# First attention of a four-layer kernel: the exponentials moved up in ScalarE's order, k, oT and v behind them, the value projection in the o bank, and both blocks of transposed P copied out by ScalarE

## The chip, the core and the metric

The program runs on one core of a Trainium2 chip. TensorE (PE) multiplies into PSUM, which the kernel addresses as eight banks of 512 fp32 columns; VectorE (DVE), ScalarE (ACT) and GpSimd (POOL) work beside it, and SyncE (SP) issues the DMAs. Every engine executes its own instructions in its own order, and the engines wait for each other on semaphores only. The metric is the device time of one execution, in microseconds (us).

## What is computed

Four layers of attention and feed-forward on x of 16 items by 256 rows by 128 features (`mod` comes from a small matrix product; `_layernorm` and `softmax` are the usual ones). The change is in the attention of the first layer, for 16 heads of 64 features:

```
h = _layernorm(x, axis=-1) * (1 + ca) + sa
x = x + ga * _L0_attn_ref(h, L0_attn_Wq, L0_attn_Wkv, L0_attn_Wo, L0_attn_bo)
...
q, k, v = heads of x @ Wq, x @ Wkv
s = jnp.einsum('bhid,bhjd->bhij', q * scale, k)
gm = jax.lax.stop_gradient(jnp.max(s, axis=-1, keepdims=True))
p = jnp.where(causal_mask, 0.0, jnp.exp(s - gm))
out = einsum('bhij,bhjd->bhid', p, v) / (jnp.sum(p, axis=-1, keepdims=True) + EPS)
return out.transpose(0, 2, 1, 3).reshape(B, N, H * Dh) @ Wo + bo
```

(The q, k, v line is shortened here.) The later layers, with their own attentions and mixtures of experts, are the same in both kernels.

## The kernel before

`attention0` works in steps. A step is one pair of heads of one item: 8 steps per item, 16 items, 128 steps with step numbers s and place p = s mod 8 in the item. `walk` calls each engine's `step(at)` for a lead-in of 6 empty steps and the first 16 steps written out, then for a hardware loop whose body (a lap) is 16 steps, then for the last 16 steps and `LAG` steps of drain. In a step, `at` is the current pair, `nx` the next, `b1`, `b2` and `b3` the pairs one, two and three steps back. The order of the calls in `step` is the order of the instructions on the engine, so the work is a software pipeline written out by hand:

- TensorE (lines 531 to 600): the transposes of P for `b2` (helper line 403), the score products of `at` (line 549), the projections of q, of v and of k for `nx` (helper lines 123 to 125, three multiplies each, because the operands are cut into two parts of reduced precision, "rounded" and "rest"), the causal mask of head 0 added into the score bank (571, 573), the product with the values for `b2` (586, "o"), the mask of head 1, and the output projection of `b3` (598, "y"). At p = 5 the transposes of the next item's normalised rows (535, "ht") come first.
- ScalarE (lines 482 to 519): the copies of oT of `b3` (498) and of the second block of transposed P (502) out of PSUM, the rounded parts of q and k for `nx` (513), v (515), and then the exponentials of head 0 and head 1 (488 and 490, two ACTIVATEs per head, each followed by a read of its row sums). At p = 5 it also writes hT (409) and its rounded part (132); at p = 3 it copies the finished sum y of an item (214).
- VectorE (lines 616 to 652): the first block of transposed P (623), the negated row maxima of both heads (628), the denominators (636, 638), the scaling of P (643, four instructions), and the rest parts of q and k (651). At p = 2 it normalises rows of a later item (172), at p = 4 it takes the statistics of the finished item (233).
- GpSimd (lines 461 to 470): three TENSOR_TENSORs per item on the sum taken at p = 3 (221, 224, 226: bias, gate, residual), and at p = 5 the rest part of hT (139).

PSUM before: banks 0 and 1 hold q and k in their first halves; the second half of bank 0 holds ht, that of bank 1 holds v. Banks 2 and 3 hold the scores of the two heads, banks 4 and 5 their transposed P (384 of 512 columns), bank 6 holds o (256 columns used), bank 7 holds y. A score product of the next step (549) waits for two things: both heads' exponentials of the step before (it overwrites the score banks), and q and k of its own pair with their rest parts.

## Time and profile before

| | us |
|---|---|
| three runs | 2811.14, 2815.62, 2815.95 |
| median | 2815.62 |
| the profiled execution, its own time | 2808.51 |
| span of its trace | 2806.8 |
| score products of the first attention, first to last start | 46.4 to 668.3 |

Over the whole span TensorE is busy 90%, VectorE 70%, ScalarE 50% and GpSimd 24%. These shares are averages over eight stages that have different limits; the change touches the first only, which lasts from about 46 to 672 us. Times in the trace count from the start of the span. The profiled execution was 7.1 us shorter than the median of the three runs.

### The profile page before, as it was taken

The page shows a single profiled execution, that of the slowest core. Times are in us where ns is not written, and L with a number is a line of the kernel's source. Part 1 is how long each engine was busy: PE and PEld are TensorE (multiplying, and loading weights), DVE is VectorE, ACT ScalarE, POOL GpSimd, SP SyncE. Part 2 cuts the span into 40 slices and gives each one's busy share as a digit, 9 for nine tenths or more (in the row PEclk, how much of TensorE's full clock was granted, in tenths as well). Part 3 has the DMA queues.
Part 4 walks back from the last instruction along what each step waited for, and adds up shares of the span by engine and source line. Part 5 has one row for each costly group of instructions (what it writes and reads, how often), then busy time and mean ns, then how long its engine had stood idle before and what let it go on. Part 6 is the DMA issues. An engine that isn't in the chain of part 4 may idle for free. (4 is left out here: it accounts for less than half of the span.)

```text
span 2806.8 us, 65268 instructions
## 1 busy us (share of the span) xinstructions
PE 2535.8 (90%) x20904; PEld 2129.8 (76%) x20904; DVE 1971.7 (70%) x6148; ACT 1416.5 (50%) x4025; POOL 660.1 (24%) x1195
## 2 busy tenths in 40 slices
PE   4999999997999989999996999968997886999888
PEld 3777777776888879999996999956665464666566
DVE  4878878786777568888885777756775225777687
ACT  3777777775555445565654322314554132555544
POOL 0000000000111100001100111146774025777322
PEclk9999999998999999999998999979998897999899
DMA  5000000002000245555554000037553754655100
GB/s 147 2 2 0 1 1 1 1 1 62 4 0 0 59 142 169 165 170 170 168 167 108 2 0 0 0 116 191 151 152 89 84 55 109 168 147 150 37 14 17
DMA packets 196168, 212.10 MB, mean 76 GB/s; under 512 B 12628, under 2 KB 179940, under 8 KB 194676
## 3 DMA queue, kind: packets, MB, share of 16 engines
q1 hardware_dynamic: 195956, 209.64, 28.2%
q8 instruction: 88, 1.44, 0.2%
q14 instruction: 124, 1.02, 0.1%
HBM read 108.95 MB, written 90.65 MB: 71 GB/s over the span
## 5 line engine op out<-in xcount | busy, mean ns | idle before, releaser
L628 DVE TENSOR_REDUCE a_nmax<-bank 128x2 f32<-128x512 f32 x256 | 164.9, 686 | 98.9 <-PE bank L549 98.9
L1098 ACT ACTIVATE a_p<-a_p,a_nmax 128x256 f32<-128x256 f32 x256 | 128.3, 502 | 209.1 <-DVE a_nmax L1286 205.3
L221 POOL TENSOR_TENSOR delta<-y,arena 128x256 f32<-128x256 f32 x32 | 24.7, 772 | 787.9 <-ACT y L214 787.9
L1734 ACT ACTIVATE a_p<-bank 128x1024 f32<-128x1024 f32 (+1 forms) x256 | 193.4, 808 | 23.7 <-PE bank L1789 19.1
L1362 ACT ACTIVATE f_silu<-bank 128x512 f32<-128x512 f32 x128 | 76.5, 597 | 214.5 <-PE bank L125 214.5
L820 ACT ACTIVATE f_hidden<-bank,arena 128x256 f32<-128x256 f32 x256 | 120.3, 472 | 114.8 <-PE bank L125 113.5
L513 ACT CAST a_qk<-bank 128x256 fp32r<-128x256 f32 x256 | 95.0, 374 | 163.3 <-PE bank L125 163.3
L883 PE MATMUL bank<-arena,f_hidden 128*128 128x128 f32 x1024 | 171.6, 288 | 6.4 <-DVE f_acc L937 5.2
L139 POOL TENSOR_TENSOR hT<-hT 128x256 fp32r<-128x256 f32 x64 | 47.0, 734 | 523.5 <-ACT hT L132 481.9
L1677 POOL TENSOR_SCALAR_AFFINE_SELECT a_p<-a_p 128x512 f32<-128x512 f32 x256 | 162.9, 636 | 0.0
L937 DVE SCALAR_TENSOR_TENSOR f_acc<-bank,f_cw,f_acc 128x128 f32<-128x128 f32 x448 | 134.8, 345 | 38.8 <-PE bank L883 36.1
L1943 DVE TENSOR_REDUCE a_nmax<-bank 128x4 f32<-128x1024 f32 x128 | 155.5, 1215 | 2.7 <-PE bank L1776 2.7
L123 PE MATMUL bank<-hT,f_w 128*128 128x256 f32 x512 | 156.0, 305 | 0.3 <-POOL hT L139 0.3
L883 PEld LDWEIGHTS bank<-arena,f_hidden 128*128 128x128 f32 x1024 | 136.6, 191 | 19.5 <-DVE f_acc L937 11.3
L124 PE MATMUL bank<-hT,f_w 128*128 128x256 f32 x512 | 145.4, 284 | 0.0
L125 PE MATMUL bank<-hT,f_w 128*128 128x256 f32 x512 | 145.3, 284 | 0.0
L1217 PE MATMUL bank<-a_v,a_pT 128*128 128x128 f32 x1024 | 138.1, 278 | 3.7 <-ACT a_pT L1081 3.6
L549 PE MATMUL bank<-a_qk 64*128 64x256 f32 x1536 | 126.2, 295 | 15.7 <-ACT a_p L490 5.4
L1217 PEld LDWEIGHTS bank<-a_v,a_pT 128*128 128x128 f32 x1024 | 131.7, 193 | 6.6 <-ACT a_pT L1081 5.4
L1417 PE MATMUL bank<-arena,f_hidden 128*128 128x128 f32 x1024 | 136.0, 276 | 0.0
L549 PEld LDWEIGHTS bank<-a_qk 64*128 64x128 f32 x1536 | 102.5, 187 | 40.7 <-DVE a_qk L651 27.4
L1292 DVE TENSOR_TENSOR a_pos<-bank,arena 128x384 f32<-128x384 f32 x256 | 130.7, 551 | 2.7 <-PE bank L125 2.4
(321 smaller groups left out, 8210.9 us busy)
## 6 DMA issues: line engine op xcount, KB each, us to landing
pos_dram<-a_pos SPq DMA_DIRECT2D x128, 383.0 KB, 2.8
a_stack<-rows_dram SPq DMA_DIRECT2D x128, 320.0 KB, 4.1
rows_dram<-a_cut SPq DMA_DIRECT2D x192, 192.0 KB, 2.4
a_shifted<-pos_dram SPq DMA_DIRECT2D x128, 256.0 KB, 2.7
f_merged<-f_staged SPq DMA_DIRECT2D x16, 578.0 KB, 9.0
gate<-gates_dram SPq DMA_DIRECT2D x32, 256.0 KB, 11.0
arena<-in_task SPq DMA_DIRECT2D x4, 1156.0 KB, 7.8
x<-in_x SPq DMA_DIRECT2D x4, 512.0 KB, 8.3
```

The lines of the kernel that those rows point to most:

```text
L123: pe.matmul(out, left[0], right[0], start=start, stop=False, skip_group_check=True)
L124: pe.matmul(out, left[0], right[1], start=False, stop=False, skip_group_check=True)
L125: return pe.matmul(out, left[1], right[0], start=False, stop=stop, skip_group_check=True)
L549: mm = pe.matmul(s_ps[h][:, t * T:(t + 1) * T], qk[64 * h:64 * h + 64, at.ring(2), 0, a, t * P:(t + 1) * P], qk[64 * h:64 * h + 64, at.rin ...
L628: dve.tensor_reduce(nmax[:, at.ring(2), h, :], s_ps[h][:].rearrange("p (t k) -> p t k", t=NT), AX_X, ALU.max, negate=True).then_inc(s["nma ...
L883: mm = pe.matmul(y, hidden[:, at.ring(2), t * P:(t + 1) * P], w["e2w"][:, at.p, :], start=(t == 0), stop=not last, skip_group_check=True)
L937: i = dve.scalar_tensor_tensor(out=a, in0=z, scalar=c[:, t, at.p:at.p + 1], in1=a, op0=ALU.mult, op1=ALU.add)
L1217: mm = pe.matmul(y[:, t * P:(t + 1) * P], pT[:, b2.ring(2), j, t * P:(t + 1) * P], v[:, slot, j, h * P:(h + 1) * P], start=(b2.p == 0 and ...
L1417: mm = pe.matmul(y_ps[at.ring(2)][:, t * P:(t + 1) * P], hidden[:, at.ring(2), c * T + t * P:c * T + (t + 1) * P], w["w3"][:, at.p, c, :], ...
L1677: pool.affine_select(blocks, blocks, [[0, 4], [1, P]], ALU.is_ge, 0.0, base=0, channel_multiplier=-1).then_inc(s["causal"], 1)
L1734: act.activation(p[:, b4.ring(2), first:end], sT_ps[:, first:end], ACT.Exp).then_inc(s["exp"], 1)
L1943: dve.tensor_reduce(nmax[:, half, 1, of], s_ps[:, 2 * T:6 * T].rearrange("p (c q) -> p c q", c=4), AX_X, ALU.max, negate=True).then_inc(s[ ...
```

## The change

In words, for each engine:

- **PSUM.** v is now projected into the second half of bank 6, beside o; ht goes into the last 128 columns of banks 4 and 5, beside transposed P.
- **ScalarE.** A step now reads: both blocks of transposed P of `b2`, rounded q, exponentials of head 0, rounded k, exponentials of head 1, oT of `b2` (of the step's own o, no longer of the one before), v. hT moves from p = 5 to p = 4, between transposed P and q, its rounded part to the end of that step. The copy of y moves from the start of p = 3 to the end of p = 2.
- **TensorE.** v is projected first, then q, then k. The v projection waits until ScalarE has copied the v and the oT before it. The ht transposes come at p = 4, and wait for nothing of q or k.
- **VectorE.** It no longer copies transposed P. Normalising and statistics go to the end of their steps, the statistics from p = 4 to p = 3; the rest of k waits for rounded k itself, and no longer for v, which came after it.
- **GpSimd.** Bias, gate and residual are written at p = 2, where the sum is taken now; `LAG` is 4.

```
-        o_ps, y_ps = k.banks[6], k.banks[7]
+        o_ps, v_ps, y_ps = k.banks[6][:, 0:T], k.banks[6][:, T:2 * T], k.banks[7]
+        ht_ps = k.psum.rearrange("p (b c) -> p b c", b=8)[:, 4:6, C:512]
...
-        LAST, LEAD, LAG = PER - 1, 6, 5
+        LAST, LEAD, LAG = PER - 1, 6, 4
...
-                    if at.p == 3 and at.shift(-4).real:
-                        biased_residual_by_pool(pool, n, at.shift(-4), k.gate[phase % 2],
+                    if at.p == 2 and at.shift(-3).real:
+                        biased_residual_by_pool(pool, n, at.shift(-3), k.gate[phase % 2],
...
                     if b2.real:
+                        wait(act, s["pT_mm"], b2, 2, 1)
+                        wait(act, s["o_mm"], b2.shift(-2))
+                        act.copy(pT[:, b2.ring(2), 0, :], pT_ps[0][:, 0:C]).then_inc(s["pT0"], 1)
                         wait(act, s["pT_mm"], b2, 2)
                         wait(act, s["o_mm"], b2.shift(-2))
                         act.copy(pT[:, b2.ring(2), 1, :], pT_ps[1][:, 0:C]).then_inc(s["pT1"], 1)
...
+                    ni = at.shift(4)
+                    if at.p == 4 and ni.real:
+                        wait(act, s["ht_mm"], ni, item=True)
+                        wait(act, s["pT0"], b2)
+                        modulated(act, k, phase, ni, ht_ps, n.hT[:, ni.s // PER % 2, :].rearrange("p (t q) -> p t q", t=NT),
+                                  s["ht"])
...
+                        rounded(nx, 0)
                     if at.real:
                         exps(0)
+                    if nx.real:
+                        rounded(nx, 1)
                     if at.real:
                         exps(1)
+                    if b2.real:
+                        wait(act, s["o_mm"], b2)
+                        wait(act, s["y_mm"], b2.shift(-2))
+                        act.copy(oT[:, b2.ring(2), :], o_ps).then_inc(s["oT"], 1)
+                    if nx.real:
+                        wait(act, s["v_mm"], nx)
+                        wait(act, s["o_mm"], nx.shift(-7 - nx.p % 2))
+                        act.copy(v[:, nx.s // 2 % 4, nx.p % 2, :], v_ps).then_inc(s["v"], 1)
+                    if at.p == 4 and ni.real:
+                        cut_hT(act, n, ni, s["ht"], s["ht_rounded"])
+                    if at.p == 2 and b3.real:
+                        take_sum(act, n, b3, y_ps, s["y_mm"], s["biased"], s["taken"])
...
-                    if at.p == 5 and ni.real:
+                    if at.p == 5:
+                        wait(pe, s["ht"], at.shift(3), item=True)
+                    ni = at.shift(4)
+                    if at.p == 4 and ni.real:
                         wait(pe, s["xn"], ni, item=True)
-                        wait(pe, s["qk"], at, 2, 1)
...
+                        wait(pe, s["v"], nx.shift(-1))
+                        wait(pe, s["oT"], b3)
+                        matmul3(pe, v_ps, halves(n.hT2, item, t * P, (t + 1) * P),
+                                [W[:, 2, part, first:first + 2 * P] for part in range(2)]).then_inc(s["v_mm"], 1)
...
-                    if b2.real:
-                        wait(dve, s["pT_mm"], b2, 2, 1)
-                        wait(dve, s["o_mm"], b2.shift(-2))
-                        dve.tensor_copy(pT[:, b2.ring(2), 0, :], pT_ps[0][:, 0:C]).then_inc(s["pT0"], 1)
...
-                    if at.p == 4 and at.shift(-5).real:
-                        row_stats(dve, n, at.shift(-5), s["added"])
...
+                    if at.p == 3 and at.shift(-4).real:
+                        row_stats(dve, n, at.shift(-4), s["added"])
```

ScalarE in a step of the loop without extras, before (from the rounded q to the second block of transposed P; L68 rows are register or semaphore instructions of `wait`):

```order
L513 CAST a_qk<-bank 128x256 [waits a0_qk_mm]
L68 REGISTER_ALU
L513 CAST a_qk<-bank 128x256 [waits a0_qk_mm]
L515 COPY a_v<-bank 128x256 [waits a0_o_mm]
L488 ACTIVATE a_p,a_sums<-bank,a_nmax 128x128 [waits a0_pT_mm,a0_masked,a0_nmax]
L490 ACTIVATE a_p,a_sums<-bank,a_nmax 128x256
L488 ACTIVATE a_p,a_sums<-bank,a_nmax 128x128 [waits a0_pT_mm,a0_masked,a0_nmax]
L490 ACTIVATE a_p,a_sums<-bank,a_nmax 128x256
L498 COPY a_oT<-bank 128x256 [waits a0_y_mm,a0_o_mm]
L502 COPY a_pT<-bank 128x384 [waits a0_o_mm,a0_pT_mm]
```

The same stretch of ScalarE's order in the changed kernel, from the second of the two copies of transposed P on (the lines are those of the changed kernel: 504 transposed P, 486 rounded q and k, 493 and 495 exponentials, 523 oT, 527 v):

```order
L504 COPY a_pT<-bank 128x384 [waits a0_o_mm,a0_pT_mm]
L68 ISA [waits a0_s_mm]
L486 CAST a_qk<-bank 128x256 [waits a0_qk_mm]
L493 ACTIVATE a_p,a_sums<-bank,a_nmax 128x128 [waits a0_pT_mm,a0_masked,a0_nmax]
L495 ACTIVATE a_p,a_sums<-bank,a_nmax 128x256
L68 REGISTER_ALU
L486 CAST a_qk<-bank 128x256 [waits a0_qk_mm]
L493 ACTIVATE a_p,a_sums<-bank,a_nmax 128x128 [waits a0_pT_mm,a0_masked,a0_nmax]
L495 ACTIVATE a_p,a_sums<-bank,a_nmax 128x256
L523 COPY a_oT<-bank 128x256 [waits a0_y_mm,a0_o_mm]
L68 REGISTER_ALU
L527 COPY a_v<-bank 128x256 [waits a0_o_mm,a0_v_mm]
```

Rounded k stands between the two heads' exponentials now, and oT and v stand behind both.

TensorE before, from the output projection at the end of p = 4 over the ht transposes to the first projection of p = 5 (`pro_mod_mm` and `pro_gate_abs` are the printed names of reused semaphores, here xn and ht):

```order
L598 MATMUL bank<-arena,a_oT 128x128 [waits a0_oT]
L598 MATMUL bank<-arena,a_oT 128x128
L68 REGISTER_ALU
L68 ISA [waits pro_mod_mm]
L535 MATMUL bank<-ident,xn 128x128 [waits a0_qk]
L535 MATMUL bank<-ident,xn 128x128
L403 MATMUL bank<-ident,a_p 128x128 [waits a0_pT1,a0_pT0,a0_p]
L403 MATMUL bank<-ident,a_p 128x128 x5
L68 REGISTER_ALU
L549 MATMUL bank<-a_qk 128x256 [waits a0_exp,a0_qk]
L549 MATMUL bank<-a_qk 128x256 x11
L123 MATMUL bank<-hT,a_W 128x256 [waits a0_qk,pro_gate_abs]
```

TensorE in the changed kernel, the same place, now one step earlier (550 is ht, 564 the scores, 612 the output projection; the last row is the first multiply of v):

```order
L612 MATMUL bank<-arena,a_oT 128x128 [waits a0_taken,a0_oT]
L612 MATMUL bank<-arena,a_oT 128x128
L68 REGISTER_ALU
L550 MATMUL bank<-ident,xn 128x128 [waits a0_pT1,a0_pT0,pro_mod_mm]
L550 MATMUL bank<-ident,xn 128x128
L403 MATMUL bank<-ident,a_p 128x128 [waits a0_pT1,a0_pT0,a0_p]
L403 MATMUL bank<-ident,a_p 128x128 x5
L68 ISA
L564 MATMUL bank<-a_qk 128x256 [waits a0_exp,a0_qk]
L564 MATMUL bank<-a_qk 128x256 x11
L68 REGISTER_ALU
L123 MATMUL bank<-a_W,hT 128x256 [waits a0_oT,a0_v]
```

The transposes no longer wait for the rest part of q, and the projections that follow wait for oT and v instead of for q and hT.

VectorE before, p = 4, from the row maxima to the first scaling of P:

```order
L628 TENSOR_REDUCE a_nmax<-bank 128x2 [waits a0_exp,a0_s_mm] x2
L233 ISA [waits a0_added]
L233 REGISTER_ALU
L233 BN_STATS row_stats<-x 128x6
L233 ISA
L233 BN_STATS row_stats<-x 128x6
L68 REGISTER_ALU
L636 TENSOR_SCALAR a_den<-a_sums 128x4 [waits a0_exp]
L638 RECIPROCAL a_rec<-a_den 128x4 [waits a0_den]
L643 TENSOR_SCALAR a_p<-a_p,a_rec 128x128 [waits a0_rec]
```

VectorE in the changed kernel, from the rest of k at the end of p = 3 into p = 4 (636 row maxima, 642 denominators, 654 rest parts):

```order
L654 TENSOR_TENSOR a_qk<-bank,a_qk 128x256 [waits a0_qk_rounded]
L233 ISA [waits a0_added]
L233 REGISTER_ALU
L233 BN_STATS row_stats<-x 128x6
L233 ISA
L233 BN_STATS row_stats<-x 128x6
L68 REGISTER_ALU
L636 TENSOR_REDUCE a_nmax<-bank 128x2 [waits a0_exp,a0_s_mm] x2
L642 TENSOR_SCALAR a_den<-a_sums 128x4 [waits a0_exp]
```

The statistics left the stretch between the maxima and the scaling, and stand between the rest of k and the next maxima.

## Rows read from the trace of the kernel before

**Rows 1.** Busy time of each engine in a stretch, then granted clock, DMA share, GB/s.
```profile
400.00:600.00 200.00, 190.76 (x1779) 155.11 (x1777) 160.50 (x473) 141.99 (x552) 14.67 (x20) 1.00 0.00 1
```

**Rows 2.** TensorE in time order: start, us, engine, line, tiles, [idle before]; score products of s = 32 to 40, and s = 48.
```profile
204.99 0.98 PE L549 MATMUL bank<-a_qk 64*128 64x256 f32 x12
210.51 0.98 PE L549 MATMUL bank<-a_qk 64*128 64x256 f32 x12
...
219.86 0.97 PE L549 MATMUL bank<-a_qk 64*128 64x256 f32 x12
224.83 0.98 PE L549 MATMUL bank<-a_qk 64*128 64x256 f32 x12
230.26 0.97 PE L549 MATMUL bank<-a_qk 64*128 64x256 f32 x12
235.14 0.97 PE L549 MATMUL bank<-a_qk 64*128 64x256 f32 x12
239.94 0.98 PE L549 MATMUL bank<-a_qk 64*128 64x256 f32 x12 [0.24 <-ACT a_p L490]
244.62 0.98 PE L549 MATMUL bank<-a_qk 64*128 64x256 f32 x12
...
283.20 0.97 PE L549 MATMUL bank<-a_qk 64*128 64x256 f32 x12
```

**Rows 3.** ScalarE in time order, step s = 39, which has no extras.
```profile
241.50 0.37 ACT L513 CAST a_qk<-bank 128x256 fp32r<-128x256 f32 x1 [1.07 <-PE bank L125]
242.21 0.37 ACT L513 CAST a_qk<-bank 128x256 fp32r<-128x256 f32 x1 [0.33 <-PE bank L125]
242.48 0.38 ACT L515 COPY a_v<-bank 128x256 f32<-128x256 f32 x1
242.74 0.38 ACT L488 ACTIVATE a_p<-bank,a_nmax 128x128 f32<-128x128 f32 x1
...
243.54 0.38 ACT L488 ACTIVATE a_p<-bank,a_nmax 128x128 f32<-128x128 f32 x1
...
244.24 0.23 ACT L490 ACTIVATION_READ_ACCUMULATOR a_p<-bank,a_nmax 128x1 f32 x1
```

**Rows 4.** TensorE in the same step: end of the first mask, transposes of P.
```profile
242.08 0.22 PE L573 MATMUL bank<-causal_bf,ident_bf 128*128 128x128 bf16 x1
...
243.66 0.85 PE L403 MATMUL bank<-ident,a_p 128*128 128x128 f32 x6
```

**Rows 5.** VectorE in the same step: denominators, scaling of P, rest parts.
```profile
242.16 0.16 DVE L636 TENSOR_SCALAR a_den<-a_sums 128x4 f32<-128x4 f32 x1
...
242.57 1.01 DVE L643 TENSOR_SCALAR a_p<-a_p,a_rec 128x128 f32<-128x128 f32 x4
243.49 0.75 DVE L651 TENSOR_TENSOR a_qk<-bank,a_qk 128x256 fp32r<-128x256 f32 x2
```

**Rows 6.** ScalarE's copy of y, GpSimd's first and third operation, VectorE's denominators, s = 35.
```profile
219.57 0.40 ACT L214 COPY y<-bank 128x256 f32<-128x256 f32 x1
...
220.12 0.73 POOL L221 TENSOR_TENSOR delta<-y,arena 128x256 f32<-128x256 f32 x1 [27.04 <-ACT y L214]
...
221.96 0.73 POOL L226 TENSOR_TENSOR x<-x,delta 128x256 f32 x1 [0.19 <-POOL delta L224]
...
222.07 0.64 DVE L636 TENSOR_SCALAR a_den<-a_sums 128x4 f32<-128x4 f32 x1
```

**Rows 7.** Around the start of s = 37: VectorE's statistics, TensorE's ht, ScalarE's pT and hT.
```profile
227.05 0.48 DVE L233 BATCH_NORM_STATS2 row_stats<-x  x2
...
229.24 0.44 PE L535 MATMUL bank<-ident,xn 128*128 128x128 f32 x2 [0.53 <-DVE a_qk L651]
...
230.37 0.48 ACT L502 COPY a_pT<-bank 128x384 f32<-128x384 f32 x1 [0.75 <-PE bank L403]
230.75 0.57 ACT L409 ACTIVATE hT<-bank,mod 128x256 f32<-128x256 f32 x1
```

**Rows 8.** ScalarE's first instruction after the loop's branch, s = 32.
```profile
206.83 0.37 ACT L498 COPY a_oT<-bank 128x256 f32<-128x256 f32 x1 [1.96 <-issue]
```

More of the change, by code:

```diff
@@ L482, in step, with rounded @@
                     nx, b1, b2, b3 = at.shift(1), at.shift(-1), at.shift(-2), at.shift(-3)
+                    def rounded(nx, i):
+                        wait(act, s["qk_mm"], nx, 2, 1 - i)
+                        act.copy(qk[:, nx.ring(2), i, 0, :], qk_ps[i][:, 0:T]).then_inc(s["qk_rounded"], 1)
                     def exps(h):
```

38 lines of the change are left out of this document (7 added, 31 removed).

## The prediction

> **What bounds the kernel now.** I read the busy time by stretches first, then the start times of the score products, and then the engines in time order within one step. The change lives in the first attention, so only that stage counts. There TensorE is busy 190.76 of 200 us at a granted clock of 1.00 [rows 1]: whatever the change does, little more than its remaining 5% and a few waits can be won. The score products mark the steps. The first item of the lap takes 244.62 - 204.99 = 39.63 us, the second 283.20 - 244.62 = 38.58, the lap 78.21 [rows 2]. The first item's steps are 5.52 (p = 0, after the loop's branch), twice 4.68, 4.97 (p = 3), 5.43 (p = 4), 4.88 (p = 5), 4.80 (p = 6) and 4.68 (p = 7). So a plain step costs 4.68, and an item about 2 us on top for its extras.
>
> What closes a plain step? I give times in s = 39 from its score product at 239.94 [rows 2]. ScalarE is free until q is there (it idled 1.07 before 1.56), rounds k at 2.27, copies v at 2.54, starts the exponentials of head 0 at 2.80 and of head 1 at 3.60, and its last read of sums ends at 244.24 + 0.23, at 4.53 [rows 3]. The next score product starts at 4.68, 0.15 later. The other two rings are shorter: VectorE's rest parts end at 4.30 [rows 5], and TensorE starts transposing P at 3.72 [rows 4]. ScalarE's chain from k to the second exponential is what ends last, by 0.15 to 0.2.
>
> **The change, plain steps.** The first mask ends at 242.08 + 0.22, at 2.36 [rows 4]. Head 0's exponentials could start then, but stood behind k and v until 2.80. In the new order the walk is: mask 2.36; start of head 0 at 2.43 (TensorE to ScalarE takes 0.04 where the rounded k follows its multiply, and a second semaphore has to be looked at; I take 0.07); 0.80 for a head (242.74 to 243.54) gives 3.23; rounded k, slot 0.27 (242.21 to 242.48), gives 3.50; head 1 to its last read, 243.54 to 244.47, is 0.93, gives 4.43; plus 0.15 is 4.58 [rows 3]. So v's slot of 0.26 and the early start are worth 0.36, the k that now stands between the heads gives back 0.27, and **0.10 per plain step** is left.
>
> Next in line: VectorE. In s = 35 its chain was 0.47 late (denominators ended at 222.71, at 2.85, against 242.32, at 2.38, in the plain step), and the step came out at 4.97, so without that delay it would allow 4.97 - 0.47 = 4.50 [rows 2, 5, 6]. TensorE: 8 transposes before the score product of s = 37 took 230.26 - 229.24 = 1.02 for ht and P together; six take some 0.75 to 0.8 of it, and from 3.72 this gives 4.47 to 4.5 [rows 2, 4, 7]. Both lie under 4.58 by less than 0.1. That is also the most a plain step could win beyond my forecast.
>
> The new copies. The first block of transposed P costs ScalarE a slot of 0.38 (230.37 to 230.75) [rows 7]; it takes at most its 0.48 of duration. What follows the last exponential starts 0.29 before the next score product (the copy of y at 219.57, before 219.86 [rows 2, 6]). There now stand oT and v (0.27 each) and two copies of transposed P (0.38 each): the last is issued by 1.01. q is rounded after that, and later than before: the two roundings are 0.71 apart for six multiplies (241.50 to 242.21), so v's three multiplies ahead of q move it from 1.56 to 1.92 [rows 3]. hT at p = 4 adds 0.6 there and ends at 1.6: hidden. The product with the values needs transposed P only behind the first mask (2.14 to 2.36); slack 1 us. Taking that copy from VectorE gives nothing, since it ran beside the score product anyway. v's projection waits for v of the pair before: v is there at -0.29 + 0.27 + 0.38 = 0.36, the projection starts when the score products are nearly through (0.98 to their end, so at about 0.9): hidden with 0.55 of slack [rows 2, 3].
>
> **p = 4 and p = 5.** The step of 5.43 has two causes. The statistics (two, 0.4 together) stood between the maxima and the scaling of P; and the ht transposes waited 0.53 for the rest part of q, and then came ahead of the transposes of P and the score product [rows 7]. Both leave: the statistics follow the rest parts, where VectorE idles until the next score product is through (it has from 4.3 to about 5.5), and ht follows the output projection of p = 3 without that wait. p = 4 becomes 4.58, a gain of 0.85. At p = 5 TensorE waited for hT out of bank 0, which cost 0.2; hT is now read a step earlier: 4.58, gain 0.30.
>
> **p = 3.** Here the change costs. In s = 35 the denominators took 0.64 instead of 0.16 and ended at 222.71; GpSimd's third operation ended at 222.69 [rows 5, 6]. So a VectorE TENSOR_SCALAR waits out a GpSimd operation. The copy of y now stands behind oT and v, 0.54 later in ScalarE's order: at +0.25 instead of -0.29 from the score product. GpSimd follows 0.55 behind it, and its third operation 1.84 behind its first: bias 0.80, gate 1.72 to 2.45, residual 2.64 to 3.37. The denominators (2.22) are held until 2.45 and the reciprocal follows. The scaling of P, which would start at 2.63, comes 0.25 behind the denominators' end (242.32 to 242.57), which is 0.02 behind the release: 0.27 after the gate's end. The residual starts 0.19 after it: the residual is first by 0.08, and the scaling starts at 3.41. That is a delay of 0.78 instead of 0.47, and p = 3 becomes 4.50 + 0.78 = **5.28**, a loss of 0.31 in the first item. ht on TensorE (0.27) hides under it. Bounds: 4.76 if there is no collision (TensorE with ht), and 0.73 more than 5.28 if one more operation gets in between.
>
> The Trainium skill (page "SBUF — State Buffer", section "Who interferes with whom") says that a VectorE tensor_scalar and a GpSimd operation take a shared port pair for the whole instruction, and that whoever issues first holds it. By the first half the collision is certain wherever they overlap; by the second it would cost VectorE nothing if the scaling came first. The rival below takes that case up.
>
> **The rest.** After the branch ScalarE stands still for 1.96 [rows 8]. oT and v now run before the branch, so it resumes 0.5 later, but has two copies fewer to make afterwards; by the same walk its last read ends at about 5.3, and the step is 5.45 to 5.5 as before. I leave p = 0 at 5.52 in the loop, and the unexplained 0.12 at p = 6 too (4.70). Start and end of the stage keep their chains: one empty step less of drain has no work in it. Later stages are the same instructions.
>
> **Sum.** First item of a lap: 5.52 + 2 x 4.58 + 5.28 + 2 x 4.58 + 4.70 + 4.58 = 38.40, against 39.63. Second: 7 x 4.58 + 5.28 = 37.34, against 38.58. Per lap 2.47, times 8 = 19.8 us. The profiled execution (span 2806.8, own time 2808.5) would become 2788.7. It was 7.1 under the median of the runs; from the median it is 2815.6 - 19.8 = **2796**.
>
> **Rivals.** (1) The scaling of P comes ahead of GpSimd's residual, or GpSimd runs elsewhere: p = 3 at 4.76, 16 times 0.52, another 8.3 us: 2787.5. For it: the margin is 0.08. Against: both are counted from the gate's end, so that they move together. (2) Plain steps gain nothing, because ScalarE's added waits or TensorE's order (0.09 of margin) take the 0.10: 12 steps a lap, 8 laps, 9.6 us back: 2805.5. (3) Slower: v's projection waits for v. It decides when ScalarE's tail behind the last exponential is longer by more than 0.55 than I count; then each further 0.1 costs 0.1 in every step. To end 5.6 us slower the steps have to lose 25.4 us, 0.20 each, so the tail must be 0.75 longer than its 0.54. Nothing in the rows is of that size except the branch, once a lap. It would give some 2823. (4) The order as built does what the diff says on ScalarE, TensorE and VectorE, so that the change is void is excluded; a sum of small losses that leaves it within 0.2% is not.
>
> **How the numbers follow.** What a measurement can tell from no change is about 0.2%, 5.6 us. Forecast 0.52; rival 1, or rings that allow 4.50 in plain steps (7.7 us more), 0.18; rival 2 0.14; together faster 0.84. Small losses together, same, 0.10. Slower 0.06. The range takes in the low case with both parts (2780, nearly) and, above, rival 2 with a little more lost at p = 3: 2782 to 2808.
>
> **What would show it.** Score products 4.58 apart in plain steps, 5.3 at p = 3 (with denominators and the first scaling held until GpSimd's gate and residual end), 4.58 at p = 4 and 5; rounded q followed by an exponential at 2.43 with ScalarE idle a little before it; laps of 75.7. I would be wrong if the idle time ahead of the score product is still ended by ScalarE at 4.68, if v's projection is seen waiting for v, or if the loop's branch costs well over 0.85.

## The result and the profile after

| | kernel before | changed kernel |
|---|---|---|
| median of the runs, us | 2814.76 (2811.14 to 2815.95, 4 runs) | 2783.28 (2782.01 to 2786.44, 4 runs) |
| profiled execution: own time, span | 2808.51, 2806.8 | 2784.05, 2782.3 |
| score products of the first attention, first start to last start | 621.18 | 596.29 |
| from the last of them to the end of the span | 2139.2 | 2139.6 |

The ratio is 0.9892, with an interval of 0.9875 to 0.9909. The forecast of 2796 was 12.7 too high, inside its range. In the profiled executions all of the gain of 24.5 lies between the first and the last score product of the first attention; I call that time the stage. (A product is twelve multiplies; I count from the first multiply of the first product to the first multiply of the last.) The medians differ by 31.5, because the profiled execution of before was some 6 us faster than its median. For that reason I argue below from the stage.

The busy time of each engine in the stretch of [rows 1], in the changed kernel (length, then TensorE, weight loads, VectorE, ScalarE, GpSimd, granted clock, DMA share, GB/s):
```profile
400.00:600.00 200.00, 197.69 (x1856) 161.57 (x1855) 145.88 (x453) 162.56 (x618) 17.55 (x24) 1.00 0.00 1
```
TensorE is now busy 197.69 of 200 us, against 190.76. ScalarE took 162.56 against 141.99: it has the copy that VectorE had.

The score products, as in [rows 2]: the first of the stage, then s = 32 to 40, s = 48, and the last one (start, us, engine, line, tiles):
```profile
46.49 1.65 PE L564 MATMUL bank<-a_qk 64*128 64x256 f32 x12 [0.92 <-DVE a_qk L654]
...
199.45 0.98 PE L564 MATMUL bank<-a_qk 64*128 64x256 f32 x12
204.48 0.98 PE L564 MATMUL bank<-a_qk 64*128 64x256 f32 x12
209.15 0.98 PE L564 MATMUL bank<-a_qk 64*128 64x256 f32 x12
213.73 0.98 PE L564 MATMUL bank<-a_qk 64*128 64x256 f32 x12
218.77 0.98 PE L564 MATMUL bank<-a_qk 64*128 64x256 f32 x12
223.35 0.98 PE L564 MATMUL bank<-a_qk 64*128 64x256 f32 x12
227.94 0.97 PE L564 MATMUL bank<-a_qk 64*128 64x256 f32 x12
232.52 0.97 PE L564 MATMUL bank<-a_qk 64*128 64x256 f32 x12
237.10 0.97 PE L564 MATMUL bank<-a_qk 64*128 64x256 f32 x12
...
274.22 0.98 PE L564 MATMUL bank<-a_qk 64*128 64x256 f32 x12
...
642.78 0.98 PE L564 MATMUL bank<-a_qk 64*128 64x256 f32 x12
```
The differences: 5.03 (p = 0, after the branch), 4.67, 4.58, 5.04 (p = 3), 4.58 (p = 4), 4.59 (p = 5), 4.58 (p = 6), 4.58 (p = 7). The lap is 274.22 - 199.45 = 74.77, against 78.21 before and 75.74 forecast. Medians over the laps of the loop, before, then after: p = 0 behind the branch 5.48 and 5.10; p = 3 in the first item of a lap 4.97 and 5.04, in the second 4.91 and 4.97; p = 4 5.44 and 4.58; p = 5 4.88 and 4.58; plain steps 4.68 and 4.58.

ScalarE in the plain step s = 39, which begins at 232.52 (answers to [rows 3]):
```profile
234.43 0.37 ACT L486 CAST a_qk<-bank 128x256 fp32r<-128x256 f32 x1 [0.76 <-PE bank L125]
234.97 0.37 ACT L493 ACTIVATE a_p<-bank,a_nmax 128x128 f32<-128x128 f32 x1 [0.16 <-PE bank L587]
...
235.77 0.37 ACT L486 CAST a_qk<-bank 128x256 fp32r<-128x256 f32 x1
236.03 0.38 ACT L493 ACTIVATE a_p<-bank,a_nmax 128x128 f32<-128x128 f32 x1
...
236.74 0.22 ACT L495 ACTIVATION_READ_ACCUMULATOR a_p<-bank,a_nmax 128x1 f32 x1
```
From the score product: q at 1.91 (forecast 1.92), head 0 at 2.45 (2.43), after an idle time of 0.16 that the mask ends, k at 3.25 (3.23), head 1 at 3.51 (3.50), the last read ends at 4.44 (4.43), and the next score product starts at 4.58. The walk of the prediction holds to 0.02 at each of its points.

The step p = 3 (s = 35, begins at 213.73; answers to [rows 6]). ScalarE's copy of y and GpSimd's three operations:
```profile
213.97 0.42 ACT L214 COPY y<-bank 128x256 f32<-128x256 f32 x1
...
214.54 0.73 POOL L221 TENSOR_TENSOR delta<-y,arena 128x256 f32<-128x256 f32 x1 [27.40 <-ACT y L214]
215.46 0.73 POOL L224 TENSOR_TENSOR delta<-delta,gate 128x256 f32<-128x256 f32 x1 [0.19 <-POOL delta L221]
216.38 0.72 POOL L226 TENSOR_TENSOR x<-x,delta 128x256 f32 x1 [0.19 <-POOL delta L224]
```
and VectorE's denominators, reciprocal, and the four scalings together:
```profile
215.96 0.26 DVE L642 TENSOR_SCALAR a_den<-a_sums 128x4 f32<-128x4 f32 x1
216.25 0.18 DVE L644 RECIPROCAL a_rec<-a_den 128x4 f32<-128x4 f32 x1
216.46 1.44 DVE L649 TENSOR_SCALAR a_p<-a_p,a_rec 128x128 f32<-128x128 f32 x4
```
The denominators take 0.26 instead of the 0.16 of [rows 5] and end 0.03 behind the end of GpSimd's gate (216.19). The four scalings take 1.44 instead of 1.01: the first of them alone has the 0.43 on top, and it ends 0.08 after GpSimd's residual. So both collisions happened as forecast, at the places forecast, but they cost 0.10 + 0.43 = 0.53 and not 0.78. This agrees with the rule of the Trainium skill named in the prediction (page "SBUF — State Buffer", section "Who interferes with whom": between GpSimd and a VectorE instruction in a mode of two ports, the one that issues first holds the shared ports for the whole instruction): the residual starts 0.08 ahead of the scaling, and the scaling did not end before it. In which mode VectorE ran the trace does not show.

ScalarE and VectorE after the loop's branch, s = 48, score product at 274.22 (answers to [rows 8], the first instruction of each engine; [idle before]):
```profile
276.13 0.48 ACT L501 COPY a_pT<-bank 128x384 f32<-128x384 f32 x1 [1.59 <-issue]
...
275.36 1.29 DVE L636 TENSOR_REDUCE a_nmax<-bank 128x2 f32<-128x512 f32 x2 [1.49 <-PE bank L564]
```
ScalarE resumes 1.91 after the score product. In the kernel before it did so 1.84 after it at s = 32 [rows 2, 8]. Over the five branches the medians are 1.73 before and 1.91 after: 0.18 later, although the changed kernel has made two more copies by then. VectorE resumes at 1.14.

### The profile page after: what moved, and what is told of

It is laid out like the page before. It is cut to its first block and busy times, and to the rows that moved or that the text cites. A ratio compares the mean times of both kernels' runs of the same rounds, so it can differ in the third digit from the quotient of the medians.

```text
span 2782.3 us, 65655 instructions
## 1 busy us (share of the span) xinstructions
PE 2526.5 (91%) x20842; PEld 2130.7 (77%) x20904; DVE 1909.6 (69%) x6020; ACT 1460.3 (52%) x4153; POOL 659.3 (24%) x1195
## 5 line engine op out<-in xcount | busy, mean ns | idle before, releaser
L1742 ACT ACTIVATE a_p<-bank 128x1024 f32<-128x1024 f32 (+1 forms) x256 | 193.4, 808 | 24.5 <-PE bank L1797 20.5
L891 PEld LDWEIGHTS bank<-arena,f_hidden 128*128 128x128 f32 x1024 | 136.9, 192 | 19.1 <-DVE f_acc L945 11.1
L649 DVE TENSOR_SCALAR a_p<-a_p,a_rec 128x128 f32<-128x128 f32 (+1 forms) x512 | 135.3, 328 | 4.5
## 6 DMA issues: line engine op xcount, KB each, us to landing
gate<-gates_dram SPq DMA_DIRECT2D x32, 256.0 KB, 11.1
```

What stands on the lines that cost most here:

```text
L649: i = dve.tensor_scalar(c, c, rec[:, r, h, t:t + 1], None, ALU.mult)
L891: mm = pe.matmul(y, hidden[:, at.ring(2), t * P:(t + 1) * P], w["e2w"][:, at.p, :], start=(t == 0), stop=not last, skip_group_check=True)
L1742: act.activation(p[:, b4.ring(2), first:end], sT_ps[:, first:end], ACT.Exp).then_inc(s["exp"], 1)
```

## The experiments

"The stage" is the time from the first to the last score product in the profiled execution, and "rest" what lies behind. Steps are medians over the laps of the loop, p = 3 in the first item of a lap. The last column is a median of four or five runs for before, changed, both, laps of 32, no loop and fewer waits, and a single run for the others.

| kernel | stage | plain | p = 3 | p = 4 | p = 0 after branch | rest | time |
|---|---|---|---|---|---|---|---|
| before | 621.18 | 4.68 | 4.97 | 5.44 | 5.48 | 2139.2 | 2814.76 |
| changed | 596.29 | 4.58 | 5.04 | 4.58 | 5.10 | 2139.6 | 2783.28 |
| rounded k first | 589.80 | 4.53 | 5.03 | 4.52 | 5.07 | 2132.1 | 2770.41 |
| later residual | 591.31 | 4.58 | 4.68 | 4.58 | 4.98 | 2141.5 | 2780.91 |
| both | 585.19 | 4.53 | 4.69 | 4.53 | 5.06 | 2144.2 | 2777.89 |
| before, v last | 612.15 | 4.52 | 4.84 | 5.44 | 6.90 | 2141.6 | 2802.07 |
| statistics at p = 4 | 601.18 | 4.58 | 5.05 | 4.90 | 5.10 | 2135.6 | 2785.58 |
| copy back on VectorE | 607.05 | 4.58 | 5.05 | 4.58 | 6.53 | 2141.8 | 2796.9 |
| both, laps of 32 | 589.62 | 4.53 | 4.69 | 4.53 | 7.17 + 8.80 | 2142.0 | 2780.77 |
| VectorE padded with waits | 600.12 | 4.58 | 5.04 | 4.58 | 5.05 | 2139.4 | 2788.11 |
| both, no loop | 582.16 | 4.53 | 4.69 | 4.53 | 4.53 | 2138.2 | 2769.41 |
| both, fewer waits | 586.12 | 4.53 | 4.69 | 4.53 | 5.17 | 2135.0 | 2769.41 |
| both, VectorE padded with memsets | 585.67 | 4.53 | 4.68 | 4.53 | 5.22 | 2154.3 | 2788.98 |

All of them do the whole computation.

### Does it win by the early exponentials?

k_first puts both roundings ahead of both heads' exponentials again, and keeps the rest of the change:
```
                         rounded(nx, 0)
-                    if at.real:
-                        exps(0)
-                    if nx.real:
                         rounded(nx, 1)
                     if at.real:
+                        exps(0)
                         exps(1)
```


> The changed kernel with rounded k ahead of both heads' exponentials on ScalarE again (q, k, head 0, head 1, oT, v). Theory (the step is closed by ScalarE's chain, which in the changed kernel is mask, head 0, k, head 1): head 0 starts at 2.54 after the score product instead of 2.45, head 1 at 3.46 (released by the second mask, which ends at 3.38) instead of 3.50, so a plain step is 4.54 instead of 4.58 and the stage about 4 us shorter. Rival (putting the exponentials ahead of k is what wins): head 0 starts later, and the step becomes 4.67. Second rival (TensorE or VectorE closes the step): 4.58 unchanged.

The plain step came out at 4.525, and the stage 6.5 us shorter than in the changed kernel. ScalarE in s = 39 of this kernel, whose score product starts at 230.89, and then TensorE (the last of the second head's masks):
```profile
232.81 0.73 ACT L486 CAST a_qk<-bank 128x256 fp32r<-128x256 f32 x2 [0.77 <-PE bank L125]
233.43 0.37 ACT L493 ACTIVATE a_p<-bank,a_nmax 128x128 f32<-128x128 f32 x1
...
234.36 0.37 ACT L493 ACTIVATE a_p<-bank,a_nmax 128x128 f32<-128x128 f32 x1
```
```profile
234.05 0.22 PE L585 MATMUL bank<-causal_bf,ident_bf 128*128 128x128 bf16 x1
```
Head 0 starts at 2.54, 0.1 later than in the changed kernel, and head 1 at 3.47, 0.04 earlier. It is released by the second head's mask, which ends at 234.05 + 0.22, at 3.38. So k between the heads costs more than the early start brings: 6.5 us, where I had expected 4. The part of the change that its name puts first is the one that does not pay; what pays in plain steps is that v is out of the way.

### Is the collision at p = 3 what I took it for?

pool_later moves GpSimd's three operations behind VectorE's scaling, and the statistics one step later (`LAG` is 5 again, here and in the kernels built on it):
```
-                    if at.p == 2 and at.shift(-3).real:
-                        biased_residual_by_pool(pool, n, at.shift(-3), k.gate[phase % 2],
+                    if at.p == 3 and at.shift(-4).real:
+                        wait(pool, s["p"], at.shift(-1))
+                        biased_residual_by_pool(pool, n, at.shift(-4), k.gate[phase % 2],
...
-                    if at.p == 3 and at.shift(-4).real:
-                        row_stats(dve, n, at.shift(-4), s["added"])
+                    if at.p == 4 and at.shift(-5).real:
+                        row_stats(dve, n, at.shift(-5), s["added"])
```


> The changed kernel with GpSimd's three operations at p = 3 started only when VectorE has scaled P in that step (3.63 after the score product), and the statistics at the end of p = 4. Theory (p = 3 is long because VectorE's scaling waits out GpSimd's residual): denominators and scaling at their plain durations, p = 3 falls from 5.04 and 4.97 to about 4.76, where the ht transposes on TensorE hold it; other steps as they are; about 15 times 0.24 = 3.7 us less. Rival (ht or the copy of y makes p = 3 long): p = 3 stays at 5.0.

VectorE in s = 35 of this kernel (score product at 212.61), and GpSimd's first operation:
```profile
214.83 0.16 DVE L643 TENSOR_SCALAR a_den<-a_sums 128x4 f32<-128x4 f32 x1
...
215.24 1.01 DVE L650 TENSOR_SCALAR a_p<-a_p,a_rec 128x128 f32<-128x128 f32 x4
```
```profile
216.47 0.73 POOL L221 TENSOR_TENSOR delta<-y,arena 128x256 f32<-128x256 f32 x1 [30.43 <-DVE a_p L650]
```
With GpSimd elsewhere both VectorE instructions have their usual durations, 0.16 and 1.01, and the step is 4.68. The stage is 5.0 shorter, 4.4 of it at p = 3 and 0.6 in the steps after the branch. So the collision is the cause of p = 3. Of ht's transposes, which are left there, 0.10 remains visible (4.68 against 4.58); I had bounded it at 4.76.

### Both together

> Both edits of k_first and pool_later together, all work done. Theory: independent, so the stage is about 8 us shorter than in the changed kernel; ratio to the kernel before about 0.986. Rival: once k is first another ring (TensorE 4.47, VectorE 4.50) closes the step and the sum is smaller than its parts.

The ratio to before is 0.9876, with an interval of 0.9856 to 0.9896 (2777.89 against 2810.78). The stage is 11.1 shorter than in the changed kernel, of 6.5 + 5.0 = 11.5 for the two alone: they add up to within 0.4.

### Before, traced again

> The kernel before, unchanged, traced a second time. Between the two traces at hand 24.5 us left, all in the first attention, but between the medians 31.5 us. If the trace of before was a short execution by chance, its stage times will repeat to 0.1 us in the first attention and the span will be some 4 to 6 us longer in later stages, where the granted clock varies. Rival: the first attention itself varies.

This execution says nothing on the theories. It took 6098.44 us, with TensorE's instructions about twice as long: the same product of a late stage, before and then in this execution (x count, busy us, mean ns, idle before):
```profile
L883 PE MATMUL bank<-arena,f_hidden 128*128 128x128 f32 x1024 | 171.6, 288 | 6.4 <-DVE f_acc L937 5.2
```
```profile
L883 PE MATMUL bank<-arena,f_hidden 128*128 128x128 f32 x1024 | 374.2, 536 | 0.0
```
So whether the traces of before differ among themselves by a few us in the later stages was not shown in this way.

### The order of v alone

before_v_last is the kernel before, with v copied behind the exponentials. The bank is the old one, so the projection of v has to wait for the v before it, and VectorE's rest of k waits for rounded k instead of v (these two are not shown):
```
-                        wait(act, s["o_mm"], nx.shift(-7 - nx.p % 2))
-                        act.copy(v[:, nx.s // 2 % 4, nx.p % 2, :], qk_ps[1][:, T:2 * T]).then_inc(s["v"], 1)
                     if at.real:
...
                         exps(1)
+                    if nx.real:
+                        wait(act, s["qk"], nx, 2)
+                        wait(act, s["o_mm"], nx.shift(-7 - nx.p % 2))
+                        act.copy(v[:, nx.s // 2 % 4, nx.p % 2, :], qk_ps[1][:, T:2 * T]).then_inc(s["v"], 1)
```


> The kernel before with one thing moved: ScalarE copies v behind both heads' exponentials (after VectorE's rest parts, v still in bank 1), and the v projection waits for the v before it. Theory (v's slot of 0.26 ahead of the exponentials is what the plain step can win): head 0 starts at 2.54, head 1 at 3.47 behind the second mask, the plain step falls from 4.68 to 4.53, p = 3, 4 and 5 stay at 4.97, 5.44 and 4.88; some 10 us less in the stage in all. Rival (the new bank and the oT order are needed for the gain): 4.68 stays.

The plain step is 4.52 (forecast 4.53), as good as in k_first: in plain steps this one move is the whole gain. Two steps fell that I had expected to stay: p = 3 from 4.97 to 4.84, and p = 5 from 4.88 to 4.73. But the step after the branch went from 5.48 to 6.90. ScalarE there, s = 48, score product at 279.01:
```profile
281.50 0.37 ACT L498 COPY a_oT<-bank 128x256 f32<-128x256 f32 x1 [2.44 <-issue]
...
283.39 0.65 ACT L513 CAST a_qk<-bank 128x256 fp32r<-128x256 f32 x2 [1.14 <-issue]
```
ScalarE stands still twice, for 2.44 and for 1.14, and both times it waits for nothing that the profile shows. No theory of mine had that.

### The statistics

stats_p4 is the changed kernel with the statistics where they were before, between the maxima and the denominators of p = 4:
```
+                    if at.p == 4 and at.shift(-5).real:
+                        row_stats(dve, n, at.shift(-5), s["added"])
                     if b1.real:
```


> The changed kernel with the statistics back at p = 4 between the row maxima and the denominators, everything else as changed. Theory (p = 4 lost 0.85 by two causes): the statistics alone put VectorE's rest parts 0.4 later, to 4.7, and the step becomes 4.9 instead of 4.58; the other half of the old 5.44 was the ht transposes waiting for the rest of q. Rival (the statistics were hidden even before, ht alone made the step long): p = 4 stays at 4.58. p = 3 unchanged at 5.04.

VectorE in s = 36 of this kernel, from 220.20 to the next score product at 225.10:
```profile
222.43 0.48 DVE L233 BATCH_NORM_STATS2 row_stats<-x  x2
222.82 0.15 DVE L644 TENSOR_SCALAR a_den<-a_sums 128x4 f32<-128x4 f32 x1
```
The denominators start at 2.62, where without statistics they start 2.2 after the score product (2.23 in s = 35 of the changed kernel), and the step is 4.90, 0.32 over plain. So of the 0.86 won at p = 4, 0.32 is the statistics. The other 0.54 is what is left, and has the size of the wait of ht in [rows 7], 0.53; ht was not put back alone. The prediction gave the two 0.4 and 0.5.

### The copy of transposed P, and the branch

pt0_dve gives the first of the two copies back to VectorE:
```
-                        wait(act, s["pT_mm"], b2, 2, 1)
-                        wait(act, s["o_mm"], b2.shift(-2))
-                        act.copy(pT[:, b2.ring(2), 0, :], pT_ps[0][:, 0:C]).then_inc(s["pT0"], 1)
...
+                    if b2.real:
+                        wait(dve, s["pT_mm"], b2, 2, 1)
+                        wait(dve, s["o_mm"], b2.shift(-2))
+                        dve.tensor_copy(pT[:, b2.ring(2), 0, :], pT_ps[0][:, 0:C]).then_inc(s["pT0"], 1)
```


> The changed kernel with the first block of transposed P copied by VectorE again, at the start of its step. Theory (that copy ran beside the score product on either engine): plain steps stay at 4.58, p = 4 and 5 too. After the loop's branch VectorE has one copy to make before the maxima; if it is that copy which made the step after the branch 5.5 in the kernel before against 5.1 now, it comes back to 5.4 or more (five times 0.4 us); rival: the branch step stays at 5.1, because ScalarE's order set it.

Plain steps stay at 4.58: there the copy on either engine is free, as forecast. All of the 10.8 us comes from elsewhere: 7.4 from the steps after the branch (6.53), 1.5 from a single step in the written-out part (s = 2, 6.13 instead of 4.62), and 1.3 from p = 5, whose step in the first item of a lap went to 4.80. After the branch, s = 48, score product at 277.44, ScalarE and then VectorE:
```profile
279.66 0.48 ACT L501 COPY a_pT<-bank 128x384 f32<-128x384 f32 x1 [1.90 <-issue]
281.69 0.37 ACT L486 CAST a_qk<-bank 128x256 fp32r<-128x256 f32 x1 [1.55 <-issue]
```
```profile
279.56 0.56 DVE L632 COPY a_pT<-bank 128x384 f32<-128x384 f32 x1 [2.47 <-issue]
280.04 1.28 DVE L637 TENSOR_REDUCE a_nmax<-bank 128x2 f32<-128x512 f32 x2
```
Again ScalarE stops twice, and VectorE's maxima, which come 1.14 after the score product in the changed kernel, come at 2.60.

What do the stops have in common? The table of DMA queues counts packets of instructions. The queue q14 moved these in the whole run, before and then after (packets, MB, share):
```profile
q14 instruction: 124, 1.02, 0.1%
```
```profile
q14 instruction: 100, 0.82, 0.1%
```
Counted by lap of the first attention it is 10 packets of 8 KB in before, before_v_last and pt0_dve, and 5 in the changed kernel, k_first, pool_later, both and stats_p4. From this I formed a theory: ScalarE's instructions are fetched again in each lap (5 packets), and VectorE's too where its body is long, and the engine that waits for its packet stands still. The times of single packets speak for the last part. After each of the five branches of the kernel before and of the changed kernel, a packet of q14 starts 0.20 to 0.25 after the start of ScalarE's last instruction and lasts 0.31 to 0.57, and ScalarE resumes 1.28 to 1.43 after its end. The next five kernels try the rest.

both_unroll4 makes the laps 32 steps long, so that one branch step is left of the five:
```
-                walk(act, PER, 2, LEAD, LAG, step)
+                walk(act, PER, 4, LEAD, LAG, step)
```
(and the same for the other three engines)

> The kernel of both with laps of 32 steps instead of 16, in the first attention only: one backward branch instead of five. Theory (each branch costs the step behind it about 0.5 us, and the first step after entering the body some 0.1): about 2 to 2.5 us less in the stage than both, other steps unchanged, steady 4.53. Rival (longer bodies have to be fetched while they run): single steps grow as p = 6 did in the kernel before, and nothing is won.

The stage became 4.4 longer. The one branch left cost 6.9 us: the step before it took 7.17, the step behind it 8.80. TensorE around it:
```profile
344.69 0.85 PE L403 MATMUL bank<-ident,a_p 128*128 128x128 f32 x6 [2.52 <-issue]
...
348.06 0.80 PE L563 MATMUL bank<-a_qk 64*128 64x256 f32 x4 [1.86 <-issue]
```
and the instruction queues of this kernel in the whole run; q8 had 89 packets in the changed kernel:
```profile
q8 instruction: 120, 1.97, 0.3%
q14 instruction: 102, 0.84, 0.1%
```
Now TensorE, whose body of 16 steps ran through the branch without a stop, stops for 2.52 and 1.86. A lap of 32 steps is no way to save the branch.

dve_pad puts six waits that are always satisfied at the start of each VectorE step of the changed kernel:
```
+                    for done, value in (("std", 1), ("rstd", 1), ("var", 1), ("W_rounded", 6), ("W_cut", 6), ("chain", 2)):
+                        dve.wait_ge(s[done], value)
```


> The changed kernel with six waits on long satisfied semaphores at the start of each VectorE step and nothing else: no work added, and VectorE idles there. In the traces so far a loop lap has 301 or 302 VectorE records where ten instruction packets of 8 KB are read per lap and the step after the branch takes 5.5 to 6.9 us (before, before_v_last, pt0_dve), and 267 where five are read and it takes 5.0 to 5.1 (after, k_first, pool_later, both, stats_p4). Theory (the branch step became cheaper because VectorE's loop body is short enough not to be read again): with some 315 records ten packets are read again and the step after the branch rises by 0.4 to 1.8 us, all other steps stay. Rival (the copy at the head of VectorE's step is what costs): it stays at 5.1 with five packets.

VectorE has 316 records a lap, more than the 301 of before, and still there are 5 packets and a branch step of 5.05. The number of records of VectorE alone is not the criterion. (It is no count of instructions either: 96 waits a lap added 49 records.) The waits cost nothing in plain steps of the loop, 4.58, but where the steps are written out, ahead of the loop and behind it, plain ones take 4.70, and VectorE's maxima start 1.2 after the score product instead of 1.0; why only there is open. The stage is 3.8 longer than in the changed kernel, 1.6 of it in its first 16 steps.

straight is both without a loop, the 128 steps written out:
```
-                walk(act, PER, 2, LEAD, LAG, step)
+                straight(act, PER, LEAD, LAG, step)
```
(for all four engines; straight calls step for s = -LEAD and on, one after the other)

> The kernel of both with the 128 steps of the first attention written out, no loop. Theory: no branch, so the five steps of 5.06 become 4.53 and the steps of 4.64 ahead of them too: 3 us less in the stage than both. Rival (TensorE's instructions, which the loop of 16 steps keeps, now have to be read all the time, as in both_unroll4, where some steps took 0.28 more): several steps per lap get longer and at least half of the 3 us is gone.

There is no branch step any more: p = 0 is 4.53. The stage is 582.16, 3.0 shorter than in both: five times 0.53 is 2.7. TensorE's queue moved 117 packets instead of 89, about six in 16 steps, and TensorE stopped for none of them, so the rival I had named did not come. Two of its steps take 4.80 and 4.83. ScalarE in the first of them, s = 38, which runs from 224.47 to 229.27:
```profile
227.72 0.21 ACT L502 ACTIVATION_READ_ACCUMULATOR a_p<-bank,a_nmax 128x1 f32 x1
228.22 0.37 ACT L500 ACTIVATE a_p<-bank,a_nmax 128x128 f32<-128x128 f32 x1 [0.29 <-issue]
```
A stop of 0.29 between the heads, again with nothing that it waits for, and it is the whole excess. The 4.80 that before shows at p = 6, which I could not explain, ends at the same length. There, in s = 38, which runs from 235.14 to 239.94, head 1 starts 0.24 after the read ahead of it instead of 0.10, at 3.74 instead of 3.60:
```profile
238.64 0.22 ACT L490 ACTIVATION_READ_ACCUMULATOR a_p<-bank,a_nmax 128x1 f32 x1
238.88 0.37 ACT L488 ACTIVATE a_p<-bank,a_nmax 128x128 f32<-128x128 f32 x1
```
I went through all traces for such steps: 17 steps outside p = 3 that last 4.80 to 4.83 where their neighbours last 4.53 to 4.68 (6 in before, 7 in pt0_dve, 2 in both_unroll4, 2 in straight). In each of them head 1 starts late, at 3.74 to 3.77, and a packet of q14 starts 0.64 to 0.67 after that, at 4.39 to 4.43. ScalarE had resumed by then, so it did not wait for this packet. (Two more steps of 4.81, the last before the loop in k_first and in pt0_dve, have no such packet.) A late packet alone doesn't lengthen a step: in the changed kernel and in dve_long some start at 0.94 to 0.98 of a plain step that keeps its length. And the place late in the step is not needed: in straight (s = 74) and both_unroll4 (s = 102) ScalarE stopped for 0.28 and 0.33, again ending 0.65 ahead of a packet that starts at 2.9, and the step took 4.66. So these stops go together with the fetching of instructions, but what they wait for is not shown. By its median of 2769.41 its ratio to before (2809.47) is 0.9861, 0.9842 to 0.9879.

trim takes six waits out of ScalarE's step in both that others imply, as here:
```
                         wait(act, s["masked"], at, 2, 1 - h)
-                        wait(act, s["pT_mm"], at.shift(-4), 2)
```


> The kernel of both without those of ScalarE's waits that an earlier wait of ScalarE already implies (scores of two steps back before q, P's transposes of four steps back before the exponentials, o of two steps back before transposed P, o before v). Theory: ScalarE's body gets shorter, by my count to about 310 records per lap from 393, but not under the 267 that a lap of VectorE has where it is kept, so five packets per lap remain, the branch step stays near 5.06 and the plain step at 4.53, since no wait removed ends last. Rival: each semaphore instruction between the exponentials costs, and the plain step falls to 4.50.

ScalarE's records go from 393 to 341 a lap, and nothing moves: plain 4.534, branch step 5.17, stage 586.12 against 585.19. Its median (2769.41, ratio 0.9860, 0.9841 to 0.9878) is below that of both only by what lies behind the stage: 2135.0 against 2144.2, where the instructions are the same. So these medians do not rank straight, trim and both; the stage ranks them.

dve_long is both with work instead of waits to lengthen VectorE's body:
```
+                    if at.real:
+                        for j in range(7):
+                            dve.memset(filler[:, at.ring(2) * 7 + j:at.ring(2) * 7 + j + 1], 0.0)
```


> The kernel with rounded k first and the later residual, with seven one-element memsets on VectorE behind the rest parts of each step, where it has some 1.2 us without work; they write a tensor that nothing reads. VectorE's body of 16 steps gets 112 records more (267 to about 379); no other engine's changes. Theory A (a body of VectorE that is long enough has its instructions fetched again each lap, beside ScalarE's; the records of waits in the earlier padding were cheap and did not count as much): 10 instruction packets a lap on that queue instead of 5, the step of the branch 6.0 to 6.9 us instead of 5.2, plain steps 4.53 as they were. Theory B (VectorE's body length has no part in it, and what matters is the copy of transposed P, by which VectorE has to wait for TensorE early in the step behind the branch): 5 packets, the branch step stays 5.1 to 5.3, stage 585 to 587 us. If seven memsets don't fit the 1.2 us, plain steps grow with either.

Each theory was half right. There are now 10 packets a lap, and VectorE comes back late, in s = 48 at 272.12 - 270.46 = 1.66 after the score product, against 271.25 - 270.11 = 1.14 in both (dve_long, then both):
```profile
272.12 1.29 DVE L636 TENSOR_REDUCE a_nmax<-bank 128x2 f32<-128x512 f32 x2 [1.98 <-PE bank L564]
```
```profile
271.25 1.29 DVE L635 TENSOR_REDUCE a_nmax<-bank 128x2 f32<-128x512 f32 x2 [1.50 <-PE bank L563]
```
But the branch step is only 5.22, 0.16 more than in both, and ScalarE does not stop a second time:
```profile
272.60 0.48 ACT L503 COPY a_pT<-bank 128x384 f32<-128x384 f32 x1 [1.90 <-issue]
...
273.35 0.67 ACT L488 CAST a_qk<-bank 128x256 fp32r<-128x256 f32 x2
```
So 10 packets are not the price. What the two kernels with laps of 16 steps and a branch step above 6.5 share, and the others with such laps don't have, is ScalarE's second stop ahead of q. And VectorE's packets are not a matter of the attention's body alone: in dve_long the queue moved 86 packets behind the stage instead of 61, and the rest took 2154.3 instead of 2144.2, though not one instruction of it is changed. The added packets lie between 460 and 830 us behind the stage's last product, and within that stretch dve_long falls behind both by some 12 us. This suggests that the place of a loop's code in the stream of instructions matters beside its length; no run shows it by itself. What rule decides which body is fetched again, and why ScalarE's second packet comes in time in one kernel and not in another, stays open. I have no way here to move code without changing it.

## Why the prediction was right, and where its sizes were off

- **Plain steps.** Forecast 4.58, measured 4.58, by the chain that the prediction walked. Rival 2 (no gain) is out. The two rings behind it were put at 4.50 and 4.47 to 4.5; before_v_last and k_first reach 4.52 and 4.53, so no plain step could win more than 0.06 beyond the forecast.
- **p = 4 and p = 5.** Forecast 4.58 for both, measured 4.58. stats_p4 splits the gain at p = 4 into 0.32 and a rest of 0.54. Over all 16 items the step p = 4 brings 13.0 us, the largest single part of the gain, then p = 5 with 4.5. That p = 5 fell because hT is there earlier was argued, not tried alone.
- **p = 3.** The mechanism was right, and rival 1 (no collision) is out. The term of the sum that was mis-sized is the delay: "the scaling starts at 3.41", with its full 0.29 behind that. The trace shows it end at 3.46, 0.08 after GpSimd's release at 3.37: 0.25 less than counted. So the step became 5.04 and not 5.28. Of the kernel before the same could have been read: the denominators in [rows 6] end 0.02 after GpSimd's end, and not 0.16 after it. I used that 0.02 for the denominators, and not for the scaling. In all 16 items the step p = 3 lost 1.0 us together, and not 16 times 0.31, which is 5.0: that is 4.0 of the 5.1 by which the forecast of the stage was short.
- **p = 0.** "It resumes 0.5 later" was wrong: ScalarE resumed 1.91 after the score product and not at some 2.3. The stop of 1.96 is no fixed length that starts when the engine runs out of work; it ends 1.28 to 1.43 after a packet of instructions has landed, and that packet starts 0.10 after the score product where it started 0.10 before it. The copies of oT and v, which now run ahead of the branch, so moved the resumption by 0.18 in the median, and the two copies fewer behind it saved the 0.5 that the prediction gave them: from ScalarE's resumption to the next score product it is 3.19 instead of 3.7. From 1.91 the prediction's walk gives 1.91 + 2 x 0.37 + 0.27 = 2.92 for head 0 (the trace has 277.14 - 274.22 = 2.92), and the step is 5.10 and not 5.5. That is 0.4 at five branches, 2.0 us. The steps on both sides of it gave a part back: 4.65 ahead and 4.67 behind, as in before, where I had forecast 4.58.
- **p = 6.** I left 0.12 unexplained, and forecast 4.70. It is 4.58 after the change. In the kernel before ScalarE started head 1 some 0.15 late there, 0.65 ahead of a packet of instructions; the changed kernel has no such stop at p = 6. That the two belong together is a coincidence of times in 17 steps, not an experiment, and leaving the 0.12 in the sum was a guess.
- **Rival 3 (v's projection waits for v).** It didn't happen: v ends 0.39 after the score product, and the projection starts at about 0.9. The prediction's other condition, that the branch might cost well over 0.85, came true in no kernel that has both copies on ScalarE and laps of 16 steps; it did in before_v_last, pt0_dve and both_unroll4.
- **The sum.** Forecast for the profiled execution -19.8, measured -24.5. From the medians it was -31.5, the rest of which lies in how the profiled execution of before stood to its own median. The rest of the span moves between 2132.1 and 2144.2 among kernels with the same instructions there, dve_long apart. With a spread of 12 us in the rest, a difference of 0.3% between the times of two of these kernels ranks nothing.

## What to carry over

Walk one step from one engine's start to the next with durations from the trace, and list the rings right behind it: both the gain and its limit then come out to a few hundredths of a microsecond. When an edit has several parts, try each alone; here one of them (k between the two exponentials) took back 6.5 us of what the others brought, and moving GpSimd's work out from under VectorE's scaling was worth another 5.0. An instruction that is held by another engine ends shortly after the release: count the wait up to the release, not the wait and then the whole instruction.

## What I had not expected of the hardware

- After the branch of a loop with laps of 16 steps, ScalarE waited for nothing visible for 1.4 to 2.6 us, and in two kernels a second time for 1.1 to 1.9 us. It goes with packets of instructions on DMA queues (5 or 10 of 8 KB a lap); in before and in the changed kernel it resumed 1.28 to 1.43 after such a packet had landed. By the medians of the table the step of the branch costs 0.4 over a plain one at the least, 2.4 at the most, and nothing where the loop is written out.
- In code without a branch ScalarE now and then lost 0.15 to 0.3 us between two instructions without waiting for a semaphore (steps of 4.80 among steps of 4.68, 4.58 and 4.53). A packet of instructions started 0.65 after it had gone on.
- TensorE goes through the branch of a lap of 16 steps without a stop (692 matrix records a lap), stops twice, for 2.52 and 1.86 us, at the branch of a lap of 32, and stops nowhere in the 128 steps written out.
- Seven one-element memsets a step on VectorE, in time that it had to spare, cost the first attention 0.5 us. In the one trace of that kernel the stages behind it took 10 us more, where no instruction was changed.
